# Two MoE passes around attention: first expert product two tiles ahead, and another order of GpSimd's row scatters

## The reference

```
x = x + 0.5 * ffn(layernorm(x))
x = x + attention(layernorm(x))
x = x + 0.5 * ffn(layernorm(x))
```

```
logits = t @ Wr.T + br ; top_v, top_i = top_k(logits, 2) ; w = softmax(top_v)
h = relu(t @ W1[e].T + b1[e])          # 128 -> 512
o = h @ W2[e].T + b2[e]                # 512 -> 128
ffn = gamma * normalised(t + w1*o[e1] + w2*o[e2]) + beta
```

## Time and profile before

| what | us |
|---|---|
| three executions, median | 656.39 |
| the profiled execution | 657.03 |
| its span, first to last instruction | 655.3 |
| TensorE busy, share of the span | 586.6, 90% |
| DVE busy | 452.0, 69% |
| ScalarE busy | 441.4, 67% |
| GpSimd busy | 388.8, 59% |
| mean granted clock of TensorE | 0.954 |

### The profile page before, as it was taken

One profiled execution on the slowest core, in us unless ns is written; L12 is line 12 of the kernel. 1 busy time (PEld: TensorE's weight loads), 2 busy tenths in 40 slices (PEclk: granted clock), 3 DMA queues, 4 the chain that ended last, 5 costly groups with the idle time before them and its releaser, 6 DMA issues.

```text
span 655.3 us, 16513 instructions
## 1 busy us (share of the span) xinstructions
PE 586.6 (90%) x4362; PEld 538.8 (82%) x4362; DVE 452.0 (69%) x1421; ACT 441.4 (67%) x1146; POOL 388.8 (59%) x481
## 2 busy tenths in 40 slices
PE   5987999999998888899898999798999959999945
PEld 5877999999998677787796888687999959998911
DVE  4775788446685989699689868956567534477635
ACT  4755666676667586768885975775876636877724
POOL 3006565657577785587424575784577777655623
PEclk9587999999999999899999999997999998999968
DMA  8902223223234110000000000112233323621051
GB/s 249 313 23 58 78 74 75 79 77 88 74 72 84 44 30 9 18 24 26 2 1 2 12 30 25 42 44 57 65 75 88 104 66 84 210 79 40 29 192 65
DMA packets 41881, 45.96 MB, mean 70 GB/s; under 512 B 8726, under 2 KB 32706, under 8 KB 41536
## 3 DMA queue, kind: packets, MB, share of 16 engines
q1 hardware_dynamic: 32496, 27.13, 14.2%
q0 software_dynamic: 9088, 17.75, 9.8%
q10 hardware_dynamic: 208, 0.02, 0.0%
HBM read 25.95 MB, written 19.83 MB: 70 GB/s over the span
## 4 chain that ended last, share of the span: by engine, by line
PE 47%; DVE 21%; POOL 10%; issue 9%; ACT 8%; DMA 3%; DVEq 0%; ACTq 0%; SPq 0%; POOLq 0%
PE banks L1066 16%; PE banks L1076 15%; DVE nb L1829 6%; DVE scratch L1836 3%; POOL rows L494 3%; POOL results L518 2%; PE banks L1163 2%; PE banks L1059 2%; PE banks L954 2%; PE banks L956 2%; PE banks L955 2%; DVE st_r L1326 1%; POOL rs L475 1%; ACT scratch L780 1%; POOL zb L507 1%
## 5 line engine op out<-in xcount | busy, mean ns | idle before, releaser
L1066 PE MATMUL banks<-scratch 128*128 128x128 f32 x1248 | 171.2, 281 | 1.5 <-ACT scratch L698 0.9
L1076 PE MATMUL banks<-blocks,scratch 128*128 x1248 | 167.1, 277 | 2.4 <-ACT scratch L705 1.3
L1579 DVE TENSOR_SCALAR scratch<-banks,blocks 128x128 f32<-128x128 f32 x312 | 95.0, 345 | 98.4 <-PE banks L1066 88.0
L1066 PEld LDWEIGHTS banks<-scratch 128*128 128x128 f32 x1248 | 156.3, 197 | 5.0 <-issue 4.5
L1076 PEld LDWEIGHTS banks<-blocks,scratch 128*128 128x128 f32 x1248 | 152.7, 193 | 4.5 <-issue 4.0
L486 POOL DMA_INDIRECT scratch<-xrows,rowbuf x78 | 75.2, 964 | 82.7 <-DVE rowbuf L1474 41.8
L692 ACT ACTIVATE scratch<-banks 128x128 f32<-128x128 f32 x156 | 43.2, 277 | 102.8 <-PE banks L1059 99.2
L780 ACT ACTIVATE scratch<-banks,nb 128x1024 f32<-128x1024 f32 x64 | 71.4, 1116 | 47.5 <-DVE nb L1829 47.1
L518 POOL DMA_INDIRECT results<-scratch x78 | 79.2, 1015 | 37.7 <-issue 20.1
L705 ACT ACTIVATE scratch<-banks,blocks 128x128 f32<-128x128 f32 x312 | 96.8, 365 | 2.5 <-PE banks L1066 2.0
L698 ACT ACTIVATE scratch<-blocks 128x512 f32 x156 | 97.2, 623 | 0.3
(11 more groups left out here) (264 smaller groups left out, 879.5 us busy)
## 6 DMA issues: line engine op xcount, KB each, us to landing
scratch<-rows SPq DMA_DIRECT2D x78, 64.5 KB, 2.0
yrows<-scratch SPq DMA_DIRECT2D x78, 64.0 KB
scratch<-in_L_ffn_W_dram SPq DMA_DIRECT2D x1, 2048.0 KB, 21.2
xrows<-tgt SPq DMA_DIRECT2D x4, 512.0 KB, 4.0
x<-in_L_attn_x_dram SPq DMA_DIRECT2D x3, 512.0 KB, 8.5
scratch<-xrows,rowbuf POOLq DMA_INDIRECT x78
results<-scratch POOLq DMA_INDIRECT x78
rows<-padrows SPq DMA_DIRECT2D x18, 64.5 KB
```

What stands on the lines that cost most here:

```text
L1066: ins = pe.matmul(hT_at(T, c), staged(T, c), xT_of(T), start=True, stop=True)
L1076: ins = pe.matmul(y_at(T), hT_of(T, c), blocks[:, W2_AT + c * D:][:, bass.ds(at, D)], start=(c == 0), stop=(c == FC - 1))
L1579: ins = dve.tensor_scalar(hT_of(T, c), hT_at(T, c), blocks[:, B1_AT + c:][:, bass.ds(at, 1)], 0.0, ALU.add, ALU.max)
```

## The change

The tile pipeline gets deeper. In step s TensorE's order is now first s+2, transpose s+4, second s. The buffers of the transposed tile, W1 and h are threefold, and h of a tile has one PSUM bank of four. The relu of a tile is no longer split over two engines: ScalarE makes all four blocks of even tiles, DVE all four of odd ones. In a step ScalarE copies and stages s+4 and then, if s is even, makes the relu of s+2; DVE adds s-1 and, if s is odd, makes the relu of s+2. The first product signals once per tile. The loops begin at step -4 (DVE -3).

On GpSimd, eight scatters of batch 2 instead of three stand ahead of `rstd`, none between it and the first send, and the other eight follow sends 0 to 7. Batch 3's scatters follow sends 12 to 19 instead of 16 to 23.

```diff
-        xt, xT, w1s, hT, ys = lent(RING * ROW), lent(2 * P), lent(2 * F), lent(2 * F), lent(RING * D)
-        assert at[0] <= ATT
+        xt, xT, w1s, hT, ys = lent(RING * ROW), lent(3 * P), lent(3 * F), lent(3 * F), lent(RING * D)
+        assert at[0] <= ATT + S
...
         def hT_at(T, c):
-            return bank(2 + 2 * (T % 2) + 2 * c // FC, c % (FC // 2) * P, (c % (FC // 2) + 1) * P)
+            return bank(2 + T % 4, c * P, (c + 1) * P)
...
+        H_LEAD, X_LEAD = 2, 4
...
-        ROWS_AT = 16
+        ROWS_AT = 12
...
-            scatter(1, BATCHES - 2, range(3))
+            scatter(1, BATCHES - 2, range(8))
             rstd(n)
-            scatter(1, BATCHES - 2, range(3, 6))
             for s in range(SLOTS):
                 send(s)
-                if s < PAIRS - 6:
-                    scatter(1, BATCHES - 2, range(s + 6, s + 7))
+                if s < TB:
+                    scatter(1, BATCHES - 2, range(s + 8, s + 9))
...
             def copy_xT(T):
                 act.wait_ge(xT_ps, T + 1)
-                if T >= 2:
-                    act.wait_ge(hT_ps, 2 * T - 2)
+                if T >= 3:
+                    act.wait_ge(hT_ps, T - 2)
...
-            def relu_first(T, at):
-                act.wait_ge(hT_ps, 2 * T + 1)
-                if T >= 2:
-                    act.wait_ge(y_ps, T - 1)
-                for c in range(FC // 2):
+            def relu_even(T, at):
+                act.wait_ge(hT_ps, T + 1)
+                if T >= 3:
+                    act.wait_ge(y_ps, T - 2)
+                for c in range(FC):
                     ins = act.activation(hT_of(T, c), hT_at(T, c), ACT.Relu, bias=blocks[:, B1_AT + c:][:, bass.ds(at, 1)], scale=1.0)
-                ins.then_inc(hT_first, 1)
+                ins.then_inc(hT_even, 1)
...
-                if s + 2 < SLOTS:
-                    e_at[s + 2] = expert_offset(ACTE, s + 2)
-                    copy_xT(t + 2)
-                    stage_w1(t + 2, e_at[s + 2])
-                if 0 <= s + 1 < SLOTS:
-                    relu_first(t + 1, e_at.pop(s + 1))
+                if s + X_LEAD < SLOTS:
+                    e_at[s + X_LEAD] = expert_offset(ACTE, s + X_LEAD)
+                    copy_xT(t + X_LEAD)
+                    stage_w1(t + X_LEAD, e_at[s + X_LEAD])
+                at = e_at.pop(s + H_LEAD, None)
+                if 0 <= s + H_LEAD < SLOTS and s % 2 == 0:
+                    relu_even(t + H_LEAD, at)
...
             def second(T, at):
-                pe.wait_ge(hT_first, T + 1)
-                pe.wait_ge(hT_sb, T + 1)
+                pe.wait_ge((hT_even, hT_odd)[T % 2], T // 2 + 1)
...
-                if s + 2 < SLOTS:
-                    turn_x(t + 2)
-                    w_at[s + 2] = expert_offset(PE, s + 2)
-                if 0 <= s + 1 < SLOTS:
-                    first(t + 1)
+                if 0 <= s + H_LEAD < SLOTS:
+                    w_at[s + H_LEAD] = expert_offset(PE, s + H_LEAD)
+                    first(t + H_LEAD)
+                if s + X_LEAD < SLOTS:
+                    turn_x(t + X_LEAD)
                 if s >= 0:
                     second(t, w_at.pop(s))
...
-            def relu_rest(T, at):
-                dve.wait_ge(hT_ps, 2 * T + 2)
+            def relu_odd(T, at):
+                dve.wait_ge(hT_ps, T + 1)
...
-                if s + 2 < SLOTS:
-                    e_at[s + 2] = expert_offset(DVE, s + 2)
-                if 0 <= s + 1 < SLOTS:
-                    relu_rest(t + 1, e_at[s + 1])
+                if s + H_LEAD + 1 < SLOTS:
+                    e_at[s + H_LEAD + 1] = expert_offset(DVE, s + H_LEAD + 1)
+                if 0 <= s + H_LEAD < SLOTS and s % 2 == 1:
+                    relu_odd(t + H_LEAD, e_at[s + H_LEAD])
```

More of the change, by code:

```diff
@@ L183, in macaron_kernel @@
          gap_ready, gap_exp, cnt_ready, prefix_ps, slots_ready, table_ready, pads_sent,
-         xT_ps, xT_sb, hT_ps, hT_sb, y_ps, y_sb,
+         xT_ps, xT_sb, hT_ps, hT_odd, y_ps, y_sb,
          z_used, xn_ready, xnT_ps, xnTh_sb, xnTl_sb, qkT_ps, qkT_sb, M_ps, M_sb, xm_ps, xmh_sb, xml_sb,
@@ L204, in macaron_kernel @@
         last_done = sem("last_done")
-        hT_first = sem("hT_first")
+        hT_even = sem("hT_even")
         x_loaded = [sem(f"x_loaded{b}") for b in range(BATCHES)]
@@ L235, in xT_of @@
         def xT_of(T):
-            return xT[:, T % 2 * P:(T % 2 + 1) * P]
+            return xT[:, T % 3 * P:(T % 3 + 1) * P]
         def staged(T, c, n=1):
-            return w1s[:, T % 2 * F + c * P:T % 2 * F + (c + n) * P]
+            return w1s[:, T % 3 * F + c * P:T % 3 * F + (c + n) * P]
         def hT_at(T, c):
-            return bank(2 + 2 * (T % 2) + 2 * c // FC, c % (FC // 2) * P, (c % (FC // 2) + 1) * P)
+            return bank(2 + T % 4, c * P, (c + 1) * P)
         def hT_of(T, c):
-            return hT[:, (T % 2 * FC + c) * P:(T % 2 * FC + c + 1) * P]
+            return hT[:, (T % 3 * FC + c) * P:(T % 3 * FC + c + 1) * P]
         def y_at(T):
@@ L297, in macaron_kernel @@
         Y_BEHIND, Y_NEAR = 12, 7
+        H_LEAD, X_LEAD = 2, 4
+        assert H_LEAD % 2 == 0 and SLOTS % 2 == 0
         BETA_AT = 18
@@ L892, in _ @@
             act.wait_ge(table_ready, 1)
-            for s in range(-2, SLOTS):
+            for s in range(-X_LEAD, SLOTS):
                 step(0, s)
@@ L896, in _ @@
                     pair_gap(1)
-                if s == GSLOTS - 3:
+                if s == GSLOTS - X_LEAD - 1:
                     act.wait_ge(table_ready, 2)
@@ L1241, in _ @@
             pe.wait_ge(table_ready, 1)
-            for s in range(-2, SLOTS):
-                if s == GSLOTS - 2:
+            for s in range(-X_LEAD, SLOTS):
+                if s == GSLOTS - H_LEAD:
                     pe.wait_ge(table_ready, 2)
@@ L1572, in table @@
                 yield
-            def relu_rest(T, at):
-                dve.wait_ge(hT_ps, 2 * T + 2)
-                if T >= 2:
-                    dve.wait_ge(y_ps, T - 1)
-                for c in range(FC // 2, FC):
+            def relu_odd(T, at):
+                dve.wait_ge(hT_ps, T + 1)
+                if T >= 3:
+                    dve.wait_ge(y_ps, T - 2)
+                for c in range(FC):
                     ins = dve.tensor_scalar(hT_of(T, c), hT_at(T, c), blocks[:, B1_AT + c:][:, bass.ds(at, 1)], 0.0, ALU.add, ALU.max)
-                ins.then_inc(hT_sb, 1)
+                ins.then_inc(hT_odd, 1)
             def add_b2(T, at):
@@ L1940, in _ @@
             lows_1 = pair_lows()
-            for s in range(-2, SLOTS + 1):
+            for s in range(-H_LEAD - 1, SLOTS + 1):
                 step(0, s)
```

9 lines of the change are left out of this document (4 added, 5 removed).

## The result

The changed kernel takes 660.33 us (median of 5 runs, 658.98 to 662.28) against 656.39 before (654.89 to 657.74): ratio 1.0062, 95% interval [1.0037, 1.0087]. It is slower by 0.6%, where 652.0 was forecast. The profiled execution took 659.69 us, its span is 658.0.

The account below looks back on a forecast made before the run. TensorE bounds pass 0 (95% full); in pass 1 GpSimd's queue does from 463 to 539, then TensorE. Gains 2.3 + 2.1 = 4.4 us off the profiled 657.03 give 652.6, median-adjusted 652.0; own range 650 to 654.4.

Parts of the forecast that it names:

- Part 1: Pass 0: the deeper pipeline gives relus more slack and saves 2.3 us, bounds -1 to 3.5.
- stall at 63: Pass 0: a second product waiting until 63.09 for DVE's relu, delayed by routing; its removal gives 1.4 us.
- the stretch at 94 to 106: Pass 0: TensorE's id product follows DVE's comparisons with DVE full; its 2.5 us of loss stay.
- Part 2: Pass 1 start: eight batch 2 scatters fit the deviations wait; five (6.5 us) hidden, 1.3 given back, first send about 467.5.
- Part 3: Pass 1: batch 3's rows from step 12; last rows at 526.8 instead of 533.70, 6.9 us sooner.
- New wait for the slots: Pass 1, GpSimd's queue before batch 3's first scatter: 3.5 us, slots at 498.0 against 494.7; bounds 0 to 9.
- tile 39 free of waits: Pass 1: tile 39's load no longer waited for, ready at 532.2 while TensorE gets there at 538.6.
- about 2 us lost at each of tiles 33 to 36: Pass 1: TensorE stands about 2 us per tile, as GpSimd makes three DMAs (3.9 us) per send until step 19.
- From there to the end: Pass 1, tile 36 to y of tile 72: ends at 611.9, 2.1 us sooner, including 1.0 for low clock; later gains lost.
- D: Rival, pass 1: batch 3's scatters block the queue, low clock at steps 8 and 9, slots at 505; 660 us, chance 0.10.
- B: Rival, pass 1: no new wait, slots there by 494.7, tile 36 turned at 529.3; 648.4 us, chance 0.20.
- C: Rival, pass 1: waits at tiles 33 to 36 drop TensorE's clock, 2.4 us more lost; 655.4 us, chance 0.24.

Follow-up runs that it names:

- e3: Changed kernel with the gathers of tiles 68 to 71 moved ahead of the deviations in GpSimd's pass 0 queue; 655.67 us, ratio 0.9988 to the kernel before.
- e13: Changed kernel with gathers of tiles 68 to 71 ahead of the deviations and batch 3's rows from step 16, ordinary chip; at the expected 650.5 us.
- e15: Kernel before with eight batch 2 rows ahead, batch 3's from step 14, gathers of tiles 68 to 71 ahead of the deviations; 1.1% faster than before.
- e4: Changed kernel with batch 3's rows back at step 16, eight of batch 2's still ahead; 655.25 us, ratio 0.9973 to the kernel before.
- e2: Kernel before with only the change's new row order on GpSimd, old pipeline kept; 653.20 us, ratio 0.9952 to the kernel before.
- e1: Changed kernel with the row order undone, so the deeper pipeline alone; 661.07 us, ratio 1.0066 to the kernel before.
- e14: Kernel before with eight of batch 2's rows ahead and batch 3's from step 14, ordinary chip; 1.1% faster than before.
- e9: Changed kernel with gathers of tiles 68 to 71 ahead of the deviations and batch 3's rows from step 16, slower chip; expert passes 223 and 209 us.

## Why the prediction was wrong

Forecast: -4.4 us. The two profiled spans differ by +2.7 (the medians by +3.9). The 7.1 between them are 3.5 in pass 0, 2.0 in attention, 1.9 in pass 1 and 1.3 in the tail, less 1.6 for the earlier start.

**Part 1, -2.3 in pass 0, was +1.2: the step that failed.** Its items held in kind: no stall at 63, the stretch at 94 to 106 unchanged, 1.85 us gained up to tile 60 (0.4 to 2.1 over the five executions), and once the gathers are moved pass 0 is 2.0 us shorter than before (e3; 2.6 in e13). Of that the gathers' order alone gives the old pipeline 0.6 (e15), so the pipeline's own gain is 1.3 to 1.9 where 2.3 was put. What I left out was the other end of the moved step. A transpose two tiles sooner needs its rows two tiles sooner, and they come from GpSimd's queue, in which tile 68's gather stands behind a wait for DVE. I counted slack for the relus, which had got more, and none for the gathers, which had got less. The rows to be read were GpSimd's gather at 182.90 and TensorE's transpose at 185.90. e3 shows the cause: that order alone is worth 4.6 us in the last 17 tiles. "If TensorE is as long as before from 51 to 208, part 1 does nothing" would have been read wrongly too: two effects of 2 to 5 us lay under it.

**Part 2** came out nearly as counted. Deviations at 464.6 and first send at 467.5 were forecast; pass 1 began 1.6 us later than before, and less that they were at 464.9 and 468.1.

**Part 3** had the right mechanism and a term too small. New wait for the slots (3.5 forecast, 5.5), tile 39 free of waits, about 2 us lost at each of tiles 33 to 36 (1.4 to 1.9, and 1.1 to 1.2 at 31 and 32), no low clock there; send 20 to tile 36 took 531.05 to 535.59, 4.5 us for 4.8 put, and 4.8 at each of tiles 33 to 35; from tile 36 to y of tile 72 it took 79.7 us where 79.0 was forecast. The slots were forecast 2.2 us later and are 3.5 later in each of the five kernels with the deeper pipeline that ran on ordinary chips (see the table). That is the term mis-sized. The chain's first links were right (ScalarE at 467.6, measured 467.5 and rows turned at 472.8, measured 472.5, both less the 1.6 us). TensorE's stalls in front of the two groups of row transposes were smaller than I put, 1.05 and 1.60 for 1.8 and 1.9. What I took off again, 1.5 for slack, did not come back: counted from the start of pass 1, y of tile 7 is 0.8 us later than before, y of tile 9 3.1 and the slots 3.5. Why, I haven't tested.

The Trainium skill ("DMA: Bandwidth & Descriptors", section "Anatomy of one DMA — SWDGE (gpsimd) path") gives a DMA of GpSimd's a fixed 2.0 us and its bytes at 436 GB/s, and the prediction's estimate by it was 4.4 us from send to transpose. The section is on GpSimd's path only, and the load is SyncE's. The trace has 4.8, 4.8, 4.8 and 4.5 at tiles 33 to 36, so the estimate was low by up to 0.4, and the measured 4.8 was the better term.

**From there to the end** I held the tail unchanged. From y of tile 72 to the last send it takes 11.0 us in all five of those kernels and 10.3 in the four with the old pipeline: 0.7 that is the pipeline's. The remaining 0.6 of the 1.3 varies between executions: the tail is 42.0 to 42.6 with the one and 41.3 to 42.1 with the other.

**Attention** was taken as untouched, a term put at nothing; it was 2.0 longer. It took 240.1 to 240.6 us in each execution with one low-clock stretch, 242.2 in the two with two, 243.1 in the one with three. More than one was seen with the deeper pipeline only (three of five profiles), yet e3 and e4 have it and show one. Whether the pipeline brings them on isn't settled.

**The rivals.** D gave 660 and is the number that came, but that is chance, for its mechanism didn't happen: the slots were at 500.9 (499.3 less the 1.6 us by which pass 1 began later), the clock was not low at steps 8 and 9, and pass 0 was the larger part. B is wrong: the wait was there. C is wrong for the kernel after, with no low clock from 515 to 543, but not as a mechanism. e3 has nearly the same waits (0.6 to 1.8 us at tiles 31 to 35), and there the clock fell in the middle of them; in e2 it fell behind a single wait of 1.61 us at tile 34:
```profile
524.90:531.80 6.90, 5.09 (x25) 4.78 (x24) 3.00 (x8) 1.56 (x5) 5.38 (x6) 0.51 0.32 96
```
```profile
524.20:527.60 3.40, 3.40 (x16) 3.40 (x17) 1.21 (x3) 1.30 (x4) 2.49 (x4) 0.50 0.29 78
```
e3's pass 1 took 0.65 us more than the kernel after's, less than the 2.4 that C put. The Trainium skill ("TensorE: Matmul & The Clock Gate", section "HAM oscillation — how this bites in real kernels") tells of a kernel with bursts of some 2 us between DMA waits of 3 to 5 us, in which every burst began at the low clock. The waits that C spoke of are shorter than those, so that kernel doesn't decide it. The waits here that are as long, at tile 39 in before, e1, e4 and e13 (3.1 to 4.8 us), each have a stretch at the low clock in or right behind them, which agrees. The shorter ones went both ways: one of 2.66 us in pass 0 and one of 1.61 in e2 had such a stretch, the six of 0.7 to 1.6 in the kernel after and one of 1.42 in e14 had none.

The forecast for the two parts apart would have been -2.3 and -2.1. e2 gives -3.5 for the second alone, e1 +4.4 for the first: the change was a good half and a bad one. They would add up to +0.9, and the medians show +3.9; the 3 us between match those of pass 1 above.

## What to carry to other kernels

When a pipeline is deepened, each step moved forward needs its inputs forward too: for each queue that feeds it, take the distance between the feeding instruction and its use at every place where that queue waits for something else, not only where the trace shows idle time. A distance that equals the latency shows no wait and has no slack. And a transfer sent ahead of its data turns into a wait for everything behind it: place it where its data are ready (with the old pipeline step 14 beat 12, with the deeper one 16 beat 12; 14 wasn't run with the deeper one, nor 16 with eight rows ahead with the old), and look at this again whenever another part of the change makes the data later.

## What the runs showed that I had not expected

- Gather to transpose was 3.00 us (issue on GpSimd to TensorE's start) before and 2.98 after, where TensorE waited for it: under 0.1 us of margin, and no idle time that would have pointed at it, in a pass that is 95% full.
- A single wait of 2.66 us in a full stream was followed by 3.4 us at 1.2 GHz; the two transposes behind it came 3.01 and 2.60 us apart instead of 1.90. Six waits of 0.7 to 1.6 us, one every 3 to 3.8 us, left the clock at 2.4 GHz in one execution (the kernel after), and nearly the same ones, 0.6 to 1.8, didn't in another (e3). In e2 one wait of 1.61 us was followed by 3.4 us at 1.2 GHz.
- One extra low-clock stretch of 3.4 us in attention goes with 0.9 to 2.1 us of its time. Half of 3.4 is 1.7.
- One chip ran the kernel before in 769.5 instead of 656.6 us. In the kernel that was profiled on both (e9 and e13) all of the difference is in the expert passes, 68 and 51 us. There the order of four gathers was worth 7.0 and 4.4 us to the old pipeline, 0.1 elsewhere (e14 and e15).
